# The transposes of the normalised rows, moved from behind the projection to right behind the scores

## The reference, cut to what matters

```python
q, k, v = layernorm(x) @ W_q.T + b_q, ctx @ W_k.T + b_k, ctx @ W_v.T + b_v   # 16 heads of 16
attn = softmax(q_h @ k_h.T / 4)                      # per block and head, 128 x 128
x = x + concat(attn @ v_h) @ W_out.T + b_out         # first half: attention
xf = layernorm(x)                                    # the "rows"
logits = xf @ Wr + br; top-2 of 8 experts, softmax of the two logits as gates
out_e = (silu(xf @ W1a[e] + b) * (xf @ W1g[e] + b)) @ W2[e] + b2[e]
x = x + sum of the two chosen experts' out_e * gate  # second half: mixture of experts
```

## Time and profile before

| | us |
|---|---|
| median of 3 runs | 1198.82 (1197.69 to 1200.43) |
| the profiled execution | 1199.31 |
| its span, first to last instruction | 1197.5 |
| PE busy in the span | 1157.2 (97%) |
| DVE busy | 1002.1 (84%) |
| ACT busy | 808.5 (68%) |
| POOL busy | 631.6 (53%) |

### The profile page before, as it was taken

How to read it: one execution, slowest core, us unless ns; L and a number is a source line. 1 busy time by engine, 2 the same in 40 slices (tenths; PEclk the granted TensorE clock), 3 DMA queues, 4 the chain that set the end, 5 groups by cost and what they waited for, 6 DMA issues and landing times. The chain is left out here.

```text
span 1197.5 us, 38483 instructions
## 1 busy us (share of the span) xinstructions
PE 1157.2 (97%) x12612; PEld 1037.5 (87%) x12613; DVE 1002.1 (84%) x2946; ACT 808.5 (68%) x1642; POOL 631.6 (53%) x736
## 2 busy tenths in 40 slices
PE   6999999999999999888999999999999999999996
PEld 4677777777777777678999999999999999999996
DVE  6789999999899989888887888888888888888883
ACT  5677777777777775658666766766766666766662
POOL 6346766777666766584653434334334434434344
PEclk9999999999999999999999999999999999999998
DMA  5122333333333334546787766666766766766753
GB/s 188 38 69 92 111 111 109 103 103 106 111 110 108 105 108 136 178 145 212 189 226 215 193 165 180 185 166 178 184 169 178 183 171 178 186 168 177 186 124 36
DMA packets 107679, 176.01 MB, mean 147 GB/s; under 512 B 14176, under 2 KB 82976, under 8 KB 107424
## 3 DMA queue, kind: packets, MB, share of 16 engines
q1 hardware_dynamic: 73472, 130.45, 34.7%
q0 software_dynamic: 26592, 36.46, 15.7%
q10 hardware_dynamic: 7488, 7.47, 1.8%
HBM read 126.21 MB, written 47.60 MB: 145 GB/s over the span
## 5 line engine op out<-in xcount | busy, mean ns | idle before, releaser
L1512 POOL DMA_INDIRECT out_rows<-y_gated,block_tokens x142 | 256.3, 1805 | 365.9 <-DMA out_rows<-y_gated,block_tokens 299.0
L592 PE MATMUL bank<-block_T_hi,w_hi 128*128 128x256 f32 x1136 | 325.8, 287 | 4.4 <-DVE block_T_lo L1233 4.4
L594 PE MATMUL bank<-block_T_hi,w_lo 128*128 128x256 f32 x1136 | 319.3, 281 | 0.0
L593 PE MATMUL bank<-block_T_lo,w_hi 128*128 128x256 f32 x1136 | 319.0, 281 | 0.0
L592 PEld LDWEIGHTS bank<-block_T_hi,w_hi 128*128 128x128 f32 x1136 | 215.6, 190 | 5.9 <-DVE block_T_lo L1233 5.8
L593 PEld LDWEIGHTS bank<-block_T_lo,w_hi 128*128 128x128 f32 x1136 | 215.7, 190 | 0.0
L594 PEld LDWEIGHTS bank<-block_T_hi,w_lo 128*128 128x128 f32 x1136 | 215.3, 189 | 0.0
L1243 DVE SCALAR_TENSOR_TENSOR act<-bank,block_b,silu_a 128x256 f32<-128x256 f32 x284 | 124.3, 479 | 76.3 <-ACT silu_a L829 45.7
L848 ACT ACTIVATE act_hi<-act 128x512 fp32r<-128x512 f32 x142 | 89.8, 633 | 138.0 <-DVE act L1243 136.5
L713 ACT ACTIVATE probs_T<-bank 128x512 f32<-128x512 f32 x256 | 132.2, 602 | 66.7 <-PE bank L439 66.7
L1216 DVE TENSOR_TENSOR w_lo<-w_raw,w_hi 128x1024 fp32r<-128x1024 f32 x142 | 167.2, 1219 | 4.9 <-ACT w_hi L814 4.5
(11 more groups left out here) (178 smaller groups left out, 2517.9 us busy)
## 6 DMA issues: line engine op xcount, KB each, us to landing
w_raw<-in_L_ffn_W SPq DMA_DIRECT2D x142, 512.0 KB, 5.8
block_rows<-routed_rows SPq DMA_DIRECT2D x71, 272.0 KB, 5.0
x_in<-in_x SPq DMA_DIRECT2D x64, 128.0 KB, 2.4
ctx_T<-in_ctx SPq DMA_DIRECT2D x16, 512.0 KB, 4.2
x_res<-in_x SPq DMA_DIRECT2D x64, 128.0 KB, 2.6
out_rows<-x SPq DMA_DIRECT2D x64, 128.0 KB, 2.4
w_lo<-in_L_ffn_W ACTq DMA_DIRECT2D x8, 512.0 KB, 4.5
out_rows<-y_gated,block_tokens POOLq DMA_INDIRECT x142, 6.2
```

Of the source, the lines that this page charges most:

```text
L592: mm(dst, w1h[k][:, c, at:at + P], xh[:, k, c, :], start=(c == 0), stop=False)
L593: mm(dst, w1h[k][:, c, at:at + P], xl[:, k, c, :], start=False, stop=False)
L594: last = mm(dst, w1l[k][:, c, at:at + P], xh[:, k, c, :], start=False, stop=(c == KC - 1))
L1512: nc.gpsimd.indirect_dma_start(out=out[:, :], out_offset=bass.IndirectOffsetOnAxis(ap=tk[:, u % U, t:t + 1], axis=0), in_=yg[:, u % 2, t, ...
```

## The change

TensorE's `squares_and_out` is split. In slots up to 64 the transposes of block t-4's rows now come directly behind the scores, ahead of the q or k projection (`squares_ahead`), and are written to the upper half of bank 7. They wait for the rows and for the copy of v out of bank 7's lower half (`s_v`), and from slot 61 on for x2. The output projection follows the q or k projection directly (`out_proj`), and waits in addition for the copy of the transposes out of bank 7 (`s_nT`). The wait for `s_ct` moves to the logits. In the slots after 64 the old place and bank are kept (`last_squares`). ScalarE forms the rows of slot t+1 at the end of slot t, ahead of `ln1_norm`, instead of at the beginning of slot t+1.

```diff
+            def squares(t, dst):
+                for c in range(KC):
+                    last = nc.tensor.transpose(dst[:, c * P:(c + 1) * P], xr[:, (t - 4) % LB, c * P:(c + 1) * P], ident)
+                last.then_inc(s_t3, 1)
+
+            def squares_ahead(t):
                 if real(t - 4):
                     pe.wait_ge(s_n2, count(t - 4))
-                    pe.wait_ge(s_ct, min(t - 1, NB))
...
+                    pe.wait_ge(s_v, min(t + 4, NB))
+                    if not real(t + 3):
+                        pe.wait_ge(s_x2, count(t - 4))
+                    squares(t, bank[7][:, D:2 * D])
...
+            def out_proj(t):
                 if real(t - 3):
                     pe.wait_ge(s_cl, count(t - 3))
+                    if real(t - 4) and t <= NB:
+                        pe.wait_ge(s_nT, count(t - 4))
                     pe.wait_ge(s_v, min(t + 4, NB))
...
                 if real(t - 4):
                     pe.wait_ge(s_nT, count(t - 4))
+                    pe.wait_ge(s_ct, min(t - 1, NB))
...
+                squares_ahead(t)
                 if real(GB * g):
                     if real(t - 1):
                         pe.wait_ge(s_mT, count(t - 1))
                     qk_proj(g, q, bank[5])
-                squares_and_out(t)
+                out_proj(t)
                 ranks_and_logits(t)
...
-                if real(t - 4) and t != NB + 2:
+                if real(t - 4) and t > NB and t != NB + 2:
                     rows(t)
                 if real(t - 4):
                     act.wait_ge(s_t3, count(t - 4))
                     if real(t - 5):
                         act.wait_ge(s_lg, count(t - 5))
-                    nc.scalar.activation(nT[:].rearrange("p c n -> p (c n)"), bank[4][:, 0:D], ACT.Copy).then_inc(s_nT, 1)
+                    src = bank[7][:, D:2 * D] if t <= NB else bank[4][:, 0:D]
+                    nc.scalar.activation(nT[:].rearrange("p c n -> p (c n)"), src, ACT.Copy).then_inc(s_nT, 1)
...
                     ctx_hi(g + 1, q // 2)
+                if t < NB and real(t - 3):
+                    rows(t + 1)
                 if real(t + 10):
                     ln1_norm(t + 10)
```

More of the change, by code:

```diff
@@ L478, in before, with last_squares @@
                 pe.wait_ge(s_xl, LB)
-            def squares_and_out(t):
-                q = t % GB
+            def squares(t, dst):
[3 more added lines that the diff above has]
+            def squares_ahead(t):
                 if real(t - 4):
                     pe.wait_ge(s_n2, count(t - 4))
-                    pe.wait_ge(s_ct, min(t - 1, NB))
[L486 to L493, removed]
+                    pe.wait_ge(s_v, min(t + 4, NB))
+                    if not real(t + 3):
+                        pe.wait_ge(s_x2, count(t - 4))
+                    squares(t, bank[7][:, D:2 * D])
+            def last_squares(t):
+                if real(t - 4):
+                    pe.wait_ge(s_n2, count(t - 4))
+                    pe.wait_ge(s_ct, NB)
+                    pe.wait_ge(s_lgt, count(t - 5))
+                    if t % GB == 2 and real(t - 10):
+                        pe.wait_ge(s_tp, groups(t - 10))
+                    squares(t, bank[4][:, 0:D])
+            def out_proj(t):
                 if real(t - 3):
                     pe.wait_ge(s_cl, count(t - 3))
+                    if real(t - 4) and t <= NB:
+                        pe.wait_ge(s_nT, count(t - 4))
                     pe.wait_ge(s_v, min(t + 4, NB))
@@ L655, in _ @@
                     keep_warm(8)
-                squares_and_out(NB + 1 + k)
+                last_squares(NB + 1 + k)
+                out_proj(NB + 1 + k)
                 expert_slot(k // U, k % U, NB + 1 + k)
```

## The result

The changed kernel takes 1209.99 us (median of 6 runs, 1208.44 to 1214.41), the kernel before 1198.61 (6 runs, 1197.69 to 1200.43). The ratio is 1.0096, 95% interval 1.0083 to 1.0109: slower by 11.4 us. Forecast were 1211.3 (+12.5), range 1205.5 to 1217. The profiled execution of the changed kernel took 1209.85, its span is 1207.8.

A forecast was written before the change was run, and what follows sets the result against it. PE was taken to bound the kernel, with DVE due at once in even slots. Odd-slot waits +12.5, even slots -0.7, given back -0.9 and tail +1.6 made +12.5 us, a median of 1211.3 us, range 1205.5 to 1217.

The forecast's parts named there:

- PE is the bound, nothing behind L434 moves: Slots 4 to 64: PE sets the pace up to L434, in even slots with DVE due at once; later work keeps its distances.
- The wait for the rows: Odd slots 5 to 55: PE's transposes wait 0.53 us for rows, +0.48 per slot in 26 slots, +12.5 us.
- The matmuls themselves: PE between scores and L434: 0.23 us saved, 0.17 added behind the scores, net 0.06 saved per slot.
- Even slots: Even slots 4 to 54: no wait for rows over 0.02 us, gain 0.03 in 26 slots, -0.7 us.
- Given back: Slots 37 and 56: earlier waits of L434 are covered by the later PE, -0.9 us; slots 57 to 60: 0.
- The new wait for the copy: Slots 60 to 64: output projection waits for the transposes' copy, 0.72 us in slot 62, +1.6 in total, bounds 0.3 and 2.9.
- The sum: Whole kernel: 12.5 - 0.7 - 0.9 + 1.6 = +12.5 us, profiled execution 1211.8, predicted median 1211.3.
- Rows in time: Odd slots: no wait for rows, gain 0.06 us each, -1.6 in slots and +1.6 in tail, 1199; chance 0.05.
- Every slot waits: Even slots: rows late too, by half the odd slots' wait, 6.5 us more, 1218; chance 0.05.

The follow-up runs named there:

- all three doses: Three kernels against the kernel before: rows 1.0 us late in odd and 0.5 in even slots, +33.6 us; 0.5 in odd alone, +11.4; in time, +0.9.
- rows_before_ctx: Changed kernel with ACT forming the next slot's rows ahead of the context half instead of behind it; 1200.61 us, ratio 1.0012 to the kernel before.
- act_part_alone: Kernel before with only ACT's half of the change (next slot's rows ahead of x's normalisation), TensorE untouched; 1200.09 us, ratio 1.0006.
- rows_at_slot_start: Changed kernel with ACT's half undone, rows formed at the start of their own slot, TensorE as changed; 1233.31 us, ratio 1.0283 to the kernel before.
- old_place_from_60: Changed kernel with the transposes' old place and bank from slot 60 and no output projection wait for the copy; 1210.44 us, ratio 1.0090.
- split_stats_third: Third run of the changed kernel with rows ahead of the context half, old place from slot 60, x's statistics split over both slots; 1197.43 us, ratio 0.9978.
- split_stats_on_before: The control: kernel before with only x's statistics split over both slots; 1228.40 us, ratio 0.9997, on a chip where the kernel before took 1229.47.
- split_stats: Changed kernel, rows ahead of the context half, old place from slot 60, x's statistics split; 1233.34 us, ratio 1.0032, where the kernel before took 1229.47.

## Why the prediction was right, step by step

- *PE is the bound, nothing behind L434 moves.* Right: from L434 to the next scores slot 31 takes 3.79 us before and after. ACT's 54.6 us of waiting vanished without effect.
- *The wait for the rows.* Forecast 0.53 us in 26 odd slots; measured 1.60 - 1.08 = 0.52 in each, and all three doses followed it. Forecast for such a slot +0.48 (its terms, 0.53 - 0.06, give 0.47), measured 8.21 against 7.77, +0.44, because the matmuls saved a little more. Odd slots in sum +11.30, forecast 12.5 - 0.45 = +12.0.
- *The matmuls themselves.* Forecast 0.06 saved per slot, measured 0.08. The rows of before and after give the terms. Scores to projection: 270.72 - 270.53 = 0.19 for the transposes, as allowed; projection to the second output step 0.35 as forecast. What I had not seen is 0.03 at the logits: from their first matmul to L434 took 267.75 - 267.29 = 0.46 and takes 273.34 - 272.91 = 0.43. Before, the copy of the transposes ended at 266.77 + 0.38 = 267.15, and the logits' weight load starts 0.05 behind it; now the copy ends at 271.39, 1.5 us ahead of them. The slots with rank matmuls bear out that the copy had held the logits. There the weight load came 0.17 behind the copy's end before, so the copy held nothing, and where no wait for rows is in the way L434 came 0.05 to 0.07 earlier (4.10 before, 4.03 to 4.05 in rows_before_ctx, slots 33, 37 and 53 apart); in the odd slots without them it came 0.08 to 0.09 earlier (3.97 or 3.98 before, 3.88 to 3.90).
- *Even slots.* Forecast -0.03 each, -0.7 in sum; measured -0.08, -2.11. The size of the saving explains half; the rest is that I charged a wait of 0.02 to 0.03 for the rows, and the transposes start almost where the projection had (1.081 to 1.084 us after the slot's start, against 1.076), so that it was under 0.01.
- *Given back.* Slot 37 as forecast: 8.33 before, 8.35 after, where its like grew by 0.46 (slot 33: 7.89 to 8.35). Slot 56 too (8.40 to 7.88). But I had put slots 57 to 60 at 0 since they wait for the transfer of the maxima, and they cost 1.1 us: that transfer landed later. Slot 57 of the changed kernel, in PE's timeline:

```profile
481.56 0.39 PE L434 MATMUL bank<-minus_max_rows,ones_bf 2*128 2x512 bf16 x4 [0.90 <-DMA minus_max_rows<-minus_max_T]
```

  In the seven profiles on chips where the kernel before takes 1199 us, slots 56 to 59 take 33.4 to 35.1 us: 33.84 before, 34.31 after, 34.37 in act_part_alone, whose TensorE has the old order. The +0.5 is within that scatter and can't be laid to the change.
- *The new wait for the copy.* The mis-sized term: +1.6 forecast, the changed kernel has +0.26 from slot 60 to the first expert matmul, and taking the wait away is worth nothing measurable. The wait is about as long as forecast (0.80 us in slot 62, forecast 0.72), and slots 61 and 62 grew by 0.69 and 0.32 for the 0.7 and 0.4 forecast. Wrong is what comes behind them: forecast -0.2 in slot 63 and +0.7 for slot 64, measured -0.89 from slot 63's start to the first expert matmul. That stretch takes 18.13 us in the changed kernel and 18.12 in rows_at_slot_start, both with the new order there; with the old one it takes 19.02 in the kernel before, 19.00 in act_part_alone, 19.04 in old_place_from_60 and 18.98 in split_stats_third. So what the wait costs in two slots is given back behind them. I had charged slot 64 with the wait as if TensorE set the pace there. The rows ahead of the first expert matmul show another engine. POOL and ACT in the kernel before, then in the changed one:

```profile
533.62 0.19 POOL L1427 TENSOR_TENSOR ln_shift<-ln_minus_mean,ln_rstd 128x1 f32<-128x1 f32 x1
533.85 0.60 ACT L754 ACTIVATE rows<-x,ln_shift,ln_rstd 128x256 f32<-128x256 f32 x1 [1.33 <-POOL ln_shift L1427]
```

```profile
544.01 0.19 POOL L1446 TENSOR_TENSOR ln_shift<-ln_minus_mean,ln_rstd 128x1 f32<-128x1 f32 x1
544.24 0.60 ACT L770 ACTIVATE rows<-x,ln_shift,ln_rstd 128x256 f32<-128x256 f32 x1 [0.57 <-POOL ln_shift L1446]
```

  Both times the last rows wait for GpSimd's step, and counted from slot 60's scores that step comes at 40.7 us before and at 41.0 after, though slots 60 to 62 had grown by 1.15. GpSimd is busy for 23.1 of the 25 us from 505 to 530 us in the kernel before, and TensorE's transposes of slot 64 wait 0.83 us for rows there, 0.19 in the changed kernel: the wait for the copy only filled time in which TensorE would have stood for GpSimd. This is read from the traces; no run changed GpSimd's work. By the Trainium skill (PSUM, section "PSUM bank collisions raise a hardware error") disjoint columns of one bank are no protection, so the wait has to be there. No run here could show a collision, and as the wait costs nothing measurable, the tail's time can't decide that question as the prediction hoped.
- *The sum.* For the profiled execution 1211.8 was forecast and 1209.85 measured, 2.0 less. The terms missed by more than that, in both directions: odd slots 0.7, even slots 1.4 and the tail 1.3 lower than forecast, slots 56 to 59 some 0.9 and the start of slot 0 0.4 higher. Against the medians, +11.4 where +12.5 was forecast, the miss looks smaller because they lie 0.8 further apart than the two profiled executions. That part of the closeness is luck; the wait of 0.52 us in 26 slots is not.
- *The rivals.* "Rows in time" was made to happen by rows_before_ctx and gave what it had been given, no change (forecast 1199, ratio 1.0012), for the forecast's reason: DVE in even slots. "Every slot waits" needs rows later than they are in even slots; rows_at_slot_start shows what that looks like.

## What to carry to other kernels

Before moving work to an earlier place in a queue, compare how far its need moves with how far its input moves: here the transposes moved up by 1.50 us and their rows by 0.49. Before, the rows had been 0.48 us early in odd slots and 1.0 in even ones; what that slack didn't cover of the difference, 0.52 us in odd slots and nothing in even ones, stood on the engine that sets the pace. An engine with the longest wait is not the one to relieve unless the bound engine waits too. And when two engines are due at the same moment in every second step, a saving on one shows only after the other's extra work has been moved out of those steps.

## What the runs showed of the hardware that was not expected

On two of the four chips that the experiments ran on, the kernel before took 1229 us instead of 1199. No profile of the kernel before was taken there, but split_stats_on_before runs at its pace. Against the kernel before on a 1199 us chip its slots 4 to 55 take 23.3 us more and the stretch from slot 60 to the first expert matmul 6.4. The difference begins in slot 10, with the scatters of rows: the exponentials start late. In the timelines of PE, ACT and POOL of split_stats_on_before, slots 31 and 32:

```profile
279.92 0.39 PE L434 MATMUL bank<-minus_max_rows,ones_bf 2*128 2x512 bf16 x4
...
288.31 0.39 PE L434 MATMUL bank<-minus_max_rows,ones_bf 2*128 2x512 bf16 x4
```

```profile
281.86 2.07 ACT L713 ACTIVATE probs_T<-bank 128x512 f32<-128x512 f32 x4 [1.20 <-PE bank L439]
...
290.07 2.07 ACT L713 ACTIVATE probs_T<-bank 128x512 f32<-128x512 f32 x4 [1.69 <-PE bank L439]
```

```profile
280.21 0.96 POOL L1454 DMA_INDIRECT routed_rows<-rows,dest_i  x1 [0.30 <-issue]
...
288.42 0.97 POOL L1454 DMA_INDIRECT routed_rows<-rows,dest_i  x1 [0.31 <-issue]
```

On the 1199 us chips the exponentials follow L434 by 1.31 us in almost every slot. Here they follow it by 1.94 and 1.76, 0.63 and 0.45 late, and by 2.2 in odd slots of split_stats, 0.9 late. But in slots 11 to 53 and in 55 of all five traces of such chips they begin 0.67 to 0.76 us after the end of the slot's second scatter (281.86 - 281.17 = 0.69, 290.07 - 289.39 = 0.68). Where that scatter ends early, in slots 54 and 56 to 60, they follow L434 by 1.31 here too. On a 1199 us chip nothing of the kind shows: in slot 27 of the kernel before they start 0.89 us ahead of the scatter's end. The scatters take no longer than elsewhere. That the release of the exponentials hangs on GpSimd's indirect transfer on those chips is what the times suggest; no run moved the scatter to test it, and why some chips do it stays open.

The same rows go with the 0.3% that the versions with rows ahead of the context half lose there: their second scatter ends 5.38 to 5.41 us after the slot's start in odd slots, 5.20 to 5.23 in the control, and their odd slots are about 0.2 us longer (slot 31: 8.59 in split_stats, 8.39 in the control). Why it ends later stays open.
